# A selective-scan block with du*B made by TensorE and most of the weighing by C on GpSimd

## The chip, the cores and the metric

One core of a Trainium2 chip runs the kernel. The time is the device time of the whole program in microseconds; the profile is of one execution on the same core. The engines are TensorE (PE, its weight loads PEld), VectorE (DVE), ScalarE (ACT), GpSimd (POOL) and SyncE (SP), which issues the DMAs.

## The reference

For 4 sequences of 256 steps: a selective state-space layer (256 channels, 16 states each) that is gated by the normalised x and added to x, and then a feed-forward layer with ternary weights and 8-bit activations. The layer that the change is about, with `hidden` the context (128 numbers a step) and z the layer-normalised x:

```python
x = einsum('ed,bld->bel', in_proj_w, hidden)
u = silu(conv4(x) + conv_b)                        # depthwise, 4 taps
x_dbl = einsum('ke,bel->bkl', x_proj_w, u)         # 8 of dt, 16 of B, 16 of C
delta = softplus(dt_proj_w @ dt_lo + dt_proj_b)
dA = exp(d_t[..., None] * A)
state = state * dA + (d_t * u_t)[..., None] * B_t[:, None, :]     # for each t
y_t = einsum('ben,bn->be', state, C_t)
y = (y + D * u) * silu(z)
```

The output is x1 + ffn(layernorm(x1)), with x1 = x + y. All of the scan is in f32.

## The kernel before

The sequences are done in two groups (g) of two (b), so that a row of W = 512 numbers is two sequences of 256 steps. The 256 channels are two halves (eh) of 128 partitions. For each group there are 16 states times 2 halves, UNITS = 32 scan units, and so 64 in all; unit i has state i // 2 and half i % 2.

A unit passes four engines. **ACT** makes the decay exp(delta * A) in one of three PSUM banks (`decays`, L653; its first column in each sequence is zero, so that one scan instruction does both sequences). **POOL** makes the drive du * B for both halves of a state in one instruction of 1024 columns (`scan_drive`, L491), where B's row was spread over the partitions by a DMA from DRAM (`b_wide`). **DVE** runs the scan (`scan`, L898), an instruction of 512 columns. The state is then weighed by C's row: for 22 of the 32 states DVE does it (`weigh`, L908, 512 columns, against `cwide`, a PSUM bank that **PE** fills from three bf16 parts of C, `spread_c`, L1177), and for the ten states of POOL_C GpSimd does it (`weigh`, L501, 1024 columns, C's row by DMA). PE adds the weighed states to `ysum`, two PSUM banks with the time steps on the partitions, by four f32 transposes of 128 columns for each unit (`add_to_y`, L1156). At the end of a group DVE multiplies `ysum` by silu(z) and x is added (`gate_and_add`).

Softplus goes by proj on PE, ACT's abs, exp, relu and ln (`softplus_parts`), and four DVE or POOL operations (`deltas`, `softplus`, `deltas_rest`). DVE splits C in three parts (`split_c`). While the units of both groups run, the engines also do the conv and projections of group 1, the ternary weights (ACT rounds, PE turns, ACT copies, DVE clips: `weight_rows`, `clip_weights`) and the feed-forward layer of group 0, at unit numbers that are written out in the lists ahead of the program (PE_ROWS, PE_GATE, DVE_VAL and so on). After the last scan come the gate of group 1, its feed-forward layer, and what is left of group 0's. Each engine runs its instructions in the order of the program; work waits by semaphores, and a bank of PSUM is filled again when its read is counted (`work_tile`, `wait_read`).

## Time and profile before

| | |
|---|---|
| time, median of 3 runs | 228.26 us (226.56 to 228.98) |
| span of the profiled execution | 224.8 us |
| busy, share of the span | PE 67%, DVE 83%, POOL 61%, ACT 58% |
| mean granted clock of TensorE | 0.803 |
| first and last scan start | 26.9 us and 184.4 us |

The busy time of an engine is the time in which one of its instructions ran. A duration of PE holds its latency, so the pace of PE is read from the starts of consecutive groups. The granted clock 0.5 is 1.2 GHz and 1.0 is 2.4 GHz. An f32 matmul that isn't a transpose stands as two instructions in the trace. Idle time counts only on the engine that sets the end.

### The profile page before, as it was taken

How to read it: one execution, taken by the hardware profiler on the slowest of the kernel's cores; microseconds unless marked ns; L12 is line 12 of the kernel's file. 1: busy time of each engine (PE TensorE's matmuls, PEld its weight loads, DVE VectorE, ACT ScalarE, POOL GpSimd, SP SyncE). 2: the span in 40 equal slices, each digit the busy share in tenths (PEclk: the TensorE clock that was granted, in tenths of full speed). 3: DMA queues.
4: the chain of work that ended last, by engine and by line, in shares of the span. 5: the costliest groups of instructions: out<-in, count | busy, mean ns of one | idle time of the engine just before them, and what ended most of it. 6: DMA issues, size and time to landing. Idle time of an engine off the chain costs nothing.

```text
span 224.8 us, 2405 instructions
## 1 busy us (share of the span) xinstructions
PE 150.9 (67%) x706; PEld 92.9 (41%) x706; DVE 186.5 (83%) x284; ACT 129.3 (58%) x197; POOL 136.8 (61%) x132
## 2 busy tenths in 40 slices
PE   6983088643979197059630777926986667899983
PEld 5531054232636186048620533504435265334552
DVE  3789999998089999999999968797869998838661
ACT  2578675336585996076341758736498015376772
POOL 5036499778900999896685999999139202691000
PEclk9995559978585769758785596985589969999999
DMA  4894943261400223004003304314000000000002
GB/s 107 231 343 123 339 146 112 87 189 42 140 13 0 75 66 92 4 0 141 0 0 98 135 3 136 73 71 140 23 1 3 23 0 0 0 28 0 23 23 70
DMA packets 12689, 17.44 MB, mean 78 GB/s; under 512 B 3468, under 2 KB 9012, under 8 KB 12678
## 3 DMA queue, kind: packets, MB, share of 16 engines
q1 hardware_dynamic: 12678, 17.30, 24.5%
q8 instruction: 5, 0.08, 0.2%
q14 instruction: 6, 0.05, 0.1%
HBM read 16.11 MB, written 1.19 MB: 77 GB/s over the span
## 4 chain that ended last, share of the span: by engine, by line
DVE 19%; PE 16%; ACT 9%; issue 6%; POOL 5%; DVEq 0%; POOLq 0%; ACTq 0%
DVE wstate L908 3%; PE work L1242 2%; DVE state L898 2%; PE work L1282 2%; DVE gam L981 2%; DVE xhat L825 2%; PE decay L1067 2%; ACT decay L653 2%; DVE pool_state L898 2%; DVE wstage L976 2%; POOL drive L491 2%; ACT gT L722 2%; ACT wstage L703 1%; PE decay L1242 1%; PE work L1249 1%
## 5 line engine op out<-in xcount | busy, mean ns | idle before, releaser
L491 POOL TENSOR_TENSOR drive<-du,b_wide 128x1024 f32<-128x1024 f32 x31 | 74.2, 2407 | 2.9 <-DVE state L898 1.8
L653 ACT ACTIVATE decay<-delta,aneg 128x510 f32<-128x510 f32 x64 | 42.9, 684 | 45.9 <-DVE state L898 23.3
L898 DVE TENSOR_TENSOR_SCAN state<-decay,drive 128x512 f32<-128x512 f32 x44 | 52.4, 1208 | 0.9 <-issue 0.9
L1156 PE MATMUL ysum<-ident,wstate 128*128 128x128 f32 x176 | 32.9, 332 | 10.6 <-DVE wstate L908 10.6
L908 DVE TENSOR_TENSOR wstate<-state,cwide 128x512 f32<-128x512 f32 x44 | 29.1, 663 | 12.2 <-issue 11.8
L1156 PEld LDWEIGHTS ysum<-ident,wstate 128*128 128x128 f32 x176 | 26.1, 172 | 18.8 <-DVE wstate L908 13.8
L501 POOL TENSOR_TENSOR pool_wstate<-pool_state,c_wide 128x1024 f32<-128x1024 f32 x10 | 23.7, 2367 | 11.4 <-PE ysum L1156 8.6
L898 DVE TENSOR_TENSOR_SCAN pool_state<-decay,drive 128x512 f32<-128x512 f32 x20 | 24.3, 1214 | 0.2 <-ACT decay L653 0.2
L1067 PE MATMUL work<-ident,wstage 128*128 128x128 f32 x80 | 14.2, 331 | 11.4 <-ACT ternary L677 7.7
L1177 PE MATMUL cwide<-cparts,sel 128*128 128x512 bf16 x22 | 10.6, 483 | 15.4 <-DVE wstate L908 14.2
L1067 PEld LDWEIGHTS work<-ident,wstage 128*128 128x128 f32 x80 | 11.8, 174 | 12.7 <-ACT ternary L677 8.1
L1242 PE MATMUL work<-ternary,qT 128*128 128x512 bf16 x46 | 16.3, 445 | 1.1 <-DVE wstage L976 0.8
L1156 PE MATMUL ysum<-ident,pool_wstate 128*128 128x128 f32 x80 | 13.3, 322 | 1.6 <-POOL pool_wstate L501 1.6
L716 ACT ACTIVATE wstage<-wstage,gam 128x512 f32<-128x512 f32 x16 | 10.6, 716 | 6.0 <-DVE gam L984 6.0
L509 POOL TENSOR_TENSOR xhat<-xhat,x_in 128x1024 f32<-128x1024 f32 (+1 forms) x2 | 3.6, 1814 | 16.0 <-DVE xhat L926 12.5
L1156 PEld LDWEIGHTS ysum<-ident,pool_wstate 128*128 128x128 f32 x80 | 11.9, 171 | 2.7 <-POOL pool_wstate L501 1.9
L976 DVE SCALAR_TENSOR_TENSOR wstage<-work,gam,wstage 128x512 f32<-128x512 f32 x12 | 8.7, 744 | 4.8 <-ACT wstage L703 3.4
L1067 PE MATMUL work<-ident,xhat 128*128 128x128 f32 x24 | 6.2, 420 | 9.6 <-ACT xhat L689 5.9
L1177 PEld LDWEIGHTS cwide<-cparts,sel 128*128 128x128 bf16 x22 | 2.5, 112 | 20.4 <-DVE wstate L908 17.6
L1156 PE MATMUL ysum<-ident,skip 128*128 128x128 f32 x16 | 3.0, 352 | 10.7 <-issue 8.7
L981 DVE TENSOR_REDUCE gam<-wstage 128x1 f32<-128x1024 f32 x8 | 9.8, 1220 | 0.3
L1249 PE MATMUL work<-bias_rows,acol 9*128 9x512 bf16 x23 | 9.8, 432 | 0.0
(180 smaller groups left out, 298.7 us busy)
## 6 DMA issues: line engine op xcount, KB each, us to landing
b_wide<-bc_rows SPq DMA_DIRECT2D x16, 512.0 KB, 4.5
c_wide<-bc_rows SPq DMA_DIRECT2D x10, 256.0 KB, 3.5
x_in<-in_x SPq DMA_DIRECT2D x2, 512.0 KB, 4.9
wstage<-in_L_ffn_gate_w SPq DMA_DIRECT2D x1, 1024.0 KB, 7.8
wstage<-in_L_ffn_val_w SPq DMA_DIRECT2D x1, 1024.0 KB, 10.3
wstage<-in_L_ffn_out_w SPq DMA_DIRECT2D x1, 1024.0 KB, 9.0
ctx_in<-in_ctx SPq DMA_DIRECT2D x2, 256.0 KB, 4.4
out<-wtap SPq DMA_DIRECT2D x4, 128.0 KB, 1.7
```

Source lines behind the costliest of these rows:

```text
L491: nc.gpsimd.tensor_tensor(drive[:, m % NDR], du[:, m // NS], rows.unsqueeze(1).to_broadcast([P, EH, W]), ALU.mult).then_inc(s_drive, 1)
L501: nc.gpsimd.tensor_tensor(pool_wstate[:], pool_state[:, k % NPS], c_wide[:, k % 2].unsqueeze(1).to_broadcast([P, EH, W]), ALU.mult).then_i ...
L653: nc.scalar.activation(v[:, :, 1:L], d[:, :, 1:L], ACT.Exp, scale=aneg[:, eh, n:n + 1]).then_inc(s_decay, 1)
L898: nc.vector.tensor_tensor_scan(dst, decay[i % ND][:], drive[:, i // EH % NDR, i % EH], 0.0, ALU.mult, ALU.add).then_inc(s_scan, 1)
L908: nc.vector.tensor_tensor(wstate[:, rank(i) % NWS], state[:, rank(i) % NST], cwide[:], ALU.mult).then_inc(s_wst, 1)
L976: release(nc.vector.scalar_tensor_tensor(v, bank[:], gam[:, 3, t:t + 1], v, ALU.mult, ALU.mult), name)
L981: link(nc.vector.tensor_reduce(gam[:, 5, t:t + 1], gv[:, t], axis=AX.X, op=ALU.max, apply_absolute_value=True))
L1067: return nc.tensor.matmul(dst, lhsT=src, rhs=ident[0:src.shape[0], 0:src.shape[0]], start=True, stop=True, is_transpose=True, **flags)
L1156: last = nc.tensor.matmul(ysum[:, k, eh * P:(eh + 1) * P], lhsT=src[:, k * P:(k + 1) * P], rhs=ident[:], start=start and k % LB == 0, stop ...
L1177: nc.tensor.matmul(cwide[:], lhsT=sel[:, m % NS], rhs=cparts[:, m // NS], start=True, stop=True).then_inc(s_cwide, 1)
L1242: nc.tensor.matmul(bank[:], lhsT=qT[:, d, t * P:(t + 1) * P], rhs=wT[:, d, cols], start=d == 0, stop=False)
L1249: fill(nc.tensor.matmul(banks[TILE[name][0]], lhsT=acol[rows, t * P:(t + 1) * P], rhs=bias_rows[rows, cols], start=False, stop=True), name)
```

## The change

The scan units are cut otherwise. A slot is a pair of states for one half of the channels (32 slots), and a unit is one sequence of a slot: one scan instruction of 512 columns runs two states of 256 steps. There are 64 units as before.

- The drive is made by PE, in four PSUM banks: du is turned (`turn_du`, duT has time on the partitions), and multiplied with a diagonal matrix of B (`drives`: for each unit two f32 matmuls, one per block of 128 steps, of 256 columns). The diagonals are made by POOL, by one select of 1024 columns for each pair of states (`diagonals`, 16 in all). Decays go to SBUF.
- The weighing is on POOL (`weigh`, 1024 columns for a slot, 28 of the 32 slots), C's rows by DMA (16 of 512 KB); slots 7, 15, 23 and 31 are weighed by DVE, 1024 columns each. `spread_c` and `split_c` are gone.
- The sum is no transpose any more: `ysum` has channels on the partitions, and PE adds a slot by two f32 matmuls of 512 columns with the identity (`sums`). The D * u term is a matmul with a diagonal of D (`skips`). The gated y is turned at a group's end (`turn_y`).
- Softplus: dt's two projections are folded in one matrix (`wd`), `pre_delta` is two f32 matmuls of 512 columns over 128 rows where it was one over 8 rows, and the four terms of delta are added by PE with four f32 matmuls (`add_delta`); DVE keeps relu, one rounding and du.
- silu(z) is made by ACT straight from x (8 instructions `silu_x`), with no turned z; the normalising of x on DVE (8) and the turning on PE (16) are gone. The clips of the weights are gone (ACT uses Sign). `scales` is two small DVE instructions where it was three.
- The lists of positions are new; the group loads of x and the load of val_w stand later in SP's order.

The core of the diff:

```diff
-POOL_C = (2, 5, 8, 13, 17, 19, 21, 24, 26, 28)
-POOL_WAIT, SUM_WAIT = 3, 6
...
+NP = NS // 2
+SLOTS = NP * EH
+UNITS = SLOTS * BG
+ORDER = [(0, 0), (1, 0), (0, 1), (1, 1)] + [(p, eh) for p in range(2, NP) for eh in range(EH)]
+NSLOT = G * SLOTS
+NUNIT = G * UNITS
+ND = 4
+NDRV = 4
+NST = 3
+NPW = 2
+NDG = 3
+NCW = 3
+DVE_SLOTS = tuple(range(7, NSLOT, 8))
+DRIVE_LEAD = 3
+SUM_LAG = 5
...
+        decay = sb("decay", [P, ND, BG, 2, L])
...
+        drive = [pb(f"drive{i}", [P, BANK]) for i in range(NDRV)]
+        banks = [work[0][:], work[1][:], ysum[:, 0], ysum[:, 1], *(d[:] for d in drive)]
...
+            def load_c(k):
+                if k >= NCW:
+                    for eh in range(EH):
+                        wait_weighed(sp, slot_of((k - NCW) // NP, (k - NCW) % NP, eh))
+                rows = c_rows[k].rearrange("b n l -> (b n l)").rearrange("(a w) -> a w", a=1).to_broadcast([P, BG * 2 * L])
+                sp.dma_start(c_wide[:, k % NCW].rearrange("p b n l -> p (b n l)"), rows).then_inc(s_cload[k % NCW], 16)
...
+            def diagonals(k):
+                g, p = divmod(k, NP)
+                if p == 0:
+                    wait_read(pool, f"bt{g}")
+                if k >= NDG:
+                    pool.wait_ge(s_drive, BG * last_slot(k - NDG) + BG)
+                values = bt[:, g, p].rearrange("p t n -> p (t n)")
+                nc.gpsimd.affine_select(out=bdiag[:, k % NDG].rearrange("p t n l -> p (t n) l"),
+                                        in_=values.unsqueeze(2).to_broadcast([P, GT * 2, P]),
+                                        compare_op=ALU.is_equal, fill=0.0, base=0, pattern=[[0, GT * 2], [-1, P]],
+                                        channel_multiplier=1).then_inc(s_diag, 1)
...
+            def weigh(s):
+                g, p, _ = slot_parts(s)
+                k = g * NP + p
+                r = pool_rank(s)
+                pool.wait_ge(s_scan, BG * s + BG)
+                pool.wait_ge(s_cload[k % NCW], 16 * (k // NCW + 1))
+                if r >= NPW:
+                    pool.wait_ge(s_ysum, s - NPW + 1)
+                nc.gpsimd.tensor_tensor(flat(pool_wstate[:, r % NPW]), flat(state[:, s % NST]), flat(c_wide[:, k % NCW]),
                                         ALU.mult).then_inc(s_poolw, 1)
...
+            diagonals(0)
+            diagonals(1)
+            split_biases()
+            for s in range(NSLOT):
+                if s % EH == 0 and s // EH + 2 < G * NP:
+                    diagonals(s // EH + 2)
+                if s not in DVE_SLOTS:
+                    weigh(s)
...
+            t = wait_full(act, "wd")
+            release(nc.scalar.activation(wdT[:].rearrange("p h e -> p (h e)"), t[:], ACT.Copy), "wd")
             act.wait_ge(s_small, 16 * 4)
...
+                if i == 3:
+                    copy_delta(0, 1)
+                    turned_du(0, 1)
+                    taps(1)
...
+                nc.scalar.activation(decay[:, s % ND, :, n, 1:L], d[:, :, 1:L], ACT.Exp,
+                                     scale=aneg[:, eh, 2 * p + n:2 * p + n + 1]).then_inc(s_decay, 1)
...
+            def make_du(g, eh):
+                t = wait_full(dve, f"dl{g}{eh}")
+                wait_u(dve, g, eh)
+                if g:
+                    wait_full(dve, f"dut0{eh}")
+                nc.vector.tensor_tensor(du[:, eh], t[:], u[:, eh], ALU.mult).then_inc(s_du, 1)
...
+                nc.vector.tensor_tensor_scan(state[:, s % NST, b].rearrange("p n l -> p (n l)"),
+                                             decay[:, s % ND, b].rearrange("p n l -> p (n l)"), drive[i % NDRV][:], 0.0,
                                              ALU.mult, ALU.add).then_inc(s_scan, 1)
...
+            def weigh(s):
+                g, p, _ = slot_parts(s)
+                k = g * NP + p
+                dve.wait_ge(s_scan, BG * s + BG)
+                dve.wait_ge(s_cload[k % NCW], 16 * (k // NCW + 1))
+                if dve_rank(s):
+                    dve.wait_ge(s_ysum, DVE_SLOTS[dve_rank(s) - 1] + 1)
+                flat = lambda v: v.rearrange("p b n l -> p (b n l)")
+                nc.vector.tensor_tensor(flat(wstate[:]), flat(state[:, s % NST]), flat(c_wide[:, k % NCW]),
                                         ALU.mult).then_inc(s_wst, 1)
...
+            def gate(g, b):
+                if b == 0:
+                    dve.wait_ge(s_ysum, SLOTS * (g + 1))
+                    dve.wait_ge(s_xs, GT * (g + 1))
+                z = xs[:, g * GT + b * LB:g * GT + (b + 1) * LB]
+                nc.vector.tensor_tensor(yg[:, :, b], ysum[:, :, b * L:(b + 1) * L], z, ALU.mult).then_inc(s_gated, 1)
...
+            def scales(row, src, t0, t1, done):
+                link(nc.vector.tensor_scalar(gam[:, src, t0:t1], gam[:, src, t0:t1], FLOOR, 1.0 / QMAX, ALU.max, ALU.mult))
+                nc.vector.reciprocal(gam[:, row, t0:t1], gam[:, src, t0:t1]).then_inc(done, 1)
...
+            positive(0, 0)
+            positive(0, 1)
+            t = wait_full(dve, "bc0")
+            release(nc.vector.tensor_copy(proj[:], t[0:2 * NS, :]), "bc0")
+            rounded(0, 0)
+            make_du(0, 0)
+            release(nc.vector.tensor_copy(delta[:, 0, 0], wait_full(dve, "dl00")[:]), "dl00")
+            rounded(0, 1)
+            t = wait_full(dve, "dut00")
+            release(nc.vector.tensor_copy(duT[:, 0, :, 0], t[:].rearrange("p (t e) -> p t e", t=GT)), "dut00")
+            make_du(0, 1)
...
-            def add_to_y(src, g, eh, start):
-                for k in range(GT):
-                    last = nc.tensor.matmul(ysum[:, k, eh * P:(eh + 1) * P], lhsT=src[:, k * P:(k + 1) * P],
-                                            rhs=ident[:], start=start and k % LB == 0, stop=True,
-                                            is_transpose=True, skip_group_check=True)
-                return last
...
+            def add_delta(g, eh):
+                name = f"dl{g}{eh}"
+                t = work_tile(name)
+                pe.wait_ge(s_relu, EH * g + eh + 1)
+                nc.tensor.matmul(t[:], lhsT=ident[:], rhs=relu[:, eh], start=True, stop=False)
+                pe.wait_ge(s_expln, 2 * (EH * g + eh) + 1)
+                nc.tensor.matmul(t[:], lhsT=ident[:], rhs=mag[:, eh], start=False, stop=False)
+                pe.wait_ge(s_back, EH * g + eh + 1)
+                nc.tensor.matmul(t[:], lhsT=nident[:], rhs=back[:, eh], start=False, stop=False)
+                pe.wait_ge(s_expln, 2 * (EH * g + eh) + 2)
+                fill(nc.tensor.matmul(t[:], lhsT=ident[:], rhs=lnw[:, eh], start=False, stop=True), name)
...
+            def skips(g):
+                if g:
+                    pe.wait_ge(s_gated, BG * g)
+                else:
+                    pe.wait_ge(s_ddiag, 1)
+                for eh in range(EH):
+                    wait_u(pe, g, eh)
+                    last = nc.tensor.matmul(ysum[:, eh], lhsT=ddiag[:, eh], rhs=u[:, eh], start=True, stop=True,
+                                            skip_group_check=True)
+                last.then_inc(s_skips, 1)
...
+            def drives(i):
+                s, b = divmod(i, BG)
+                g, p, eh = slot_parts(s)
+                k = g * NP + p
+                if i >= NDRV:
+                    pe.wait_ge(s_scan, i - NDRV + 1)
+                if p == 0 and b == 0:
+                    wait_read(pe, f"dut{g}{eh}")
+                pe.wait_ge(s_diag, k + 1)
+                bank = drive[i % NDRV][:].rearrange("p (n l) -> p n l", n=2)
+                for c in range(LB):
+                    t = b * LB + c
+                    last = nc.tensor.matmul(bank[:, :, c * P:(c + 1) * P], lhsT=duT[:, g, t, eh], rhs=bdiag[:, k % NDG, t],
+                                            start=True, stop=True)
+                last.then_inc(s_drive, 1)
...
+            def sums(s):
+                _, _, eh = slot_parts(s)
+                wait_weighed(pe, s)
+                src = wstate[:] if s in DVE_SLOTS else pool_wstate[:, pool_rank(s) % NPW]
+                for n in range(2):
+                    last = nc.tensor.matmul(ysum[:, eh], lhsT=ident[:], rhs=src[:, :, n], start=False, stop=True,
+                                            skip_group_check=True)
+                last.then_inc(s_ysum, 1)
...
-            project(0)
+            t = work_tile("wd")
+            wait_read(pe, "dtw")
+            for k in range(EH):
+                last = nc.tensor.matmul(t[:, k * DI:(k + 1) * DI], lhsT=xproj[0:DR, k * P:(k + 1) * P],
+                                        rhs=dtwT[:].rearrange("p h e -> p (h e)"), start=True, stop=True)
+            fill(last, "wd")
             pre_delta(0, 0)
             pre_delta(0, 1)
+            project(0)
+            taps(1)
+            add_delta(0, 0)
+            turn_b(0)
+            turn_du(0, 0)
+            add_delta(0, 1)
+            turn_du(0, 1)
             context(1)
-            spread_c(0)
-            for name in ("pre01", "ctx1"):
+            for name in ("bt0", "wd", "xc00", "conv1"):
+                wait_read(pe, name)
+            for i in range(DRIVE_LEAD):
+                drives(i)
+            for name in ("dut01", "ctx1"):
                 wait_read(pe, name)
             skips(0)
             for i in range(PE_OUT[-1] + 1):
-                scan_step(i)
+                if i + DRIVE_LEAD < NUNIT:
+                    drives(i + DRIVE_LEAD)
+                if i >= SUM_LAG and (i - SUM_LAG) % BG == 0:
+                    s = (i - SUM_LAG) // BG
+                    if s < NSLOT - 1:
+                        if s == SLOTS:
+                            skips(1)
+                        sums(s)
                 if i < EH * TAPS:
...
+            for s in range((PE_OUT[-1] - SUM_LAG) // BG + 1, NSLOT):
+                sums(s)
+            for b in range(BG):
+                turn_y(1, b)
```

## Rows read from the trace of the kernel before

**Rows 1.** Windows: busy us of each engine, granted clock (PEclk), DMA; scans, tail, three PE stretches.

```profile
core 0: us, PE busy (x) PEld busy (x) DVE busy (x) ACT busy (x) POOL busy (x), PEclk, DMA share, GB/s
27.00:186.00 159.00, 102.30 (x467) 66.97 (x467) 140.96 (x178) 90.49 (x131) 115.80 (x69) 0.75 0.21 67
186.00:224.80 38.80, 32.52 (x187) 17.18 (x187) 24.85 (x59) 22.61 (x39) 11.07 (x37) 1.00 0.06 21
8.60:12.00 3.40, 3.40 (x11) 1.42 (x10) 3.29 (x7) 3.06 (x7) 0.00 (x0) 1.00 0.87 250
30.60:34.00 3.40, 3.40 (x6) 1.15 (x6) 3.40 (x5) 1.56 (x3) 3.40 (x3) 0.50 0.01 0
57.00:71.00 14.00, 12.54 (x38) 7.60 (x38) 8.20 (x15) 8.43 (x13) 4.68 (x4) 0.62 0.19 60
```

**Rows 2.** The page, part 5: costliest groups (busy, mean ns, idle before them).

```profile
L491 POOL TENSOR_TENSOR drive<-du,b_wide 128x1024 f32<-128x1024 f32 x31 | 74.2, 2407 | 2.9 <-DVE state L898 1.8
...
L898 DVE TENSOR_TENSOR_SCAN state<-decay,drive 128x512 f32<-128x512 f32 x44 | 52.4, 1208 | 0.9 <-issue 0.9
L1156 PE MATMUL ysum<-ident,wstate 128*128 128x128 f32 x176 | 32.9, 332 | 10.6 <-DVE wstate L908 10.6
L908 DVE TENSOR_TENSOR wstate<-state,cwide 128x512 f32<-128x512 f32 x44 | 29.1, 663 | 12.2 <-issue 11.8
...
L501 POOL TENSOR_TENSOR pool_wstate<-pool_state,c_wide 128x1024 f32<-128x1024 f32 x10 | 23.7, 2367 | 11.4 <-PE ysum L1156 8.6
L898 DVE TENSOR_TENSOR_SCAN pool_state<-decay,drive 128x512 f32<-128x512 f32 x20 | 24.3, 1214 | 0.2 <-ACT decay L653 0.2
```

**Rows 3.** Timeline, start-up: start us, us, instruction.

```profile
8.56 3.60 PE L1119 MATMUL ysum<-ctxT,wtapT 128*128 128x512 f32 x8
...
12.20 0.69 ACT L729 ACTIVATE u<-ysum,convb 128x512 f32<-128x512 f32 x1
...
12.90 1.28 ACT L730 ACT_TABLE_LOAD   x1
...
26.94 1.22 DVE L898 TENSOR_TENSOR_SCAN state<-decay,drive 128x512 f32<-128x512 f32 x1
```

**Rows 4.** Timeline of PE, 30.5 to 35 us: two taps, four instructions.

```profile
30.57 3.62 PE L1119 MATMUL work<-ctxT,wtapT 128*128 128x512 f32 x4
33.99 0.63 PE L1177 MATMUL cwide<-cparts,sel 128*128 128x512 bf16 x1
```

**Rows 5.** Timeline of PE, 104 to 107 us: 128-column transposes.

```profile
104.54 1.04 PE L1156 MATMUL ysum<-ident,pool_wstate 128*128 128x128 f32 x8
105.42 1.04 PE L1156 MATMUL ysum<-ident,wstate 128*128 128x128 f32 x8
```

**Rows 6.** Timeline of PE, 198 to 212 us: one bank of the feed-forward layer.

```profile
201.49 0.60 PE L1242 MATMUL cwide<-ternary,qT 128*128 128x512 bf16 x2
202.03 0.39 PE L1249 MATMUL cwide<-bias_rows,acol 9*128 9x512 bf16 x1
202.35 0.61 PE L1242 MATMUL work<-ternary,qT 128*128 128x512 bf16 x2
```

**Rows 7.** Instruction groups kept apart by shape: selects on POOL.

```profile
L424 POOL TENSOR_SCALAR_AFFINE_SELECT pick<-pick 128x16 bf16<-128x16 bf16 x3 | 0.6, 198 | 0.4
...
L418 POOL TENSOR_SCALAR_AFFINE_SELECT ident<-ident 128x128 f32<-128x128 f32 x1 | 0.3, 292 | 0.2 <-POOL ident L417 0.2
```

**Rows 8.** Timeline of DVE, 19 to 40 us: an operation, freely and held up.

```profile
30.36 0.48 DVE L825 TENSOR_SCALAR xhat<-x_in,mv,nv 128x256 f32<-128x256 f32 x1
...
35.33 2.56 DVE L825 TENSOR_SCALAR xhat<-x_in,mv,nv 128x256 f32<-128x256 f32 x1
```

**Rows 9.** Chain of work that ended last, 186 to 190 us: start us, us, what.

```profile
186.29 1.27 PE ysum L1156 x8
...
187.58 1.30 DVE xhat L926 x2
...
188.91 1.26 DVE xhat L930
```

More of the change, by code:

```diff
@@ L133, in work_tiles, with place @@
     tiles, used = {}, [0] * 8
-    for names, banks in ((first, (0, 1, 2, 3)), (scans, (0, 1)), (last, (4, 5, 6, 7, 0, 1))):
+    def place(name, bank):
+        tiles[name] = (bank, used[bank])
+        used[bank] += 1
+    for name, bank in first.items():
+        place(name, bank)
+    for names, banks in ((scans, (0, 1)), (last, (4, 5, 6, 7, 0, 1))):
         for i, name in enumerate(names):
-            bank = banks[i % len(banks)]
-            tiles[name] = (bank, used[bank])
-            used[bank] += 1
+            place(name, banks[i % len(banks)])
     return tiles
@@ L1001, in _ @@
+            make_du(0, 0)
[4 more added lines that the diff above has]
+            make_du(0, 1)
+            for i in range(NUNIT):
                 scan(i)
-                if i and not on_pool(i - 1):
-                    weigh(i - 1)
+                if i % BG == BG - 1 and i // BG in DVE_SLOTS:
+                    weigh(i // BG)
@@ L1122, in convolve_tap, with pre_delta @@
                     fill(last, name)
+            def pre_delta(g, eh):
+                name = f"pre{g}{eh}"
+                t = work_tile(name)
+                if g == 0:
+                    wait_read(pe, "wd")
+                for k in (1, 0):
+                    wait_u(pe, g, k)
+                    last = nc.tensor.matmul(t[:], lhsT=wdT[:, k, eh * P:(eh + 1) * P], rhs=u[:, k], start=k == 1,
+                                            stop=k == 0)
+                fill(last, name)
             def project(g):
-                name = f"proj{g}"
+                name = f"bc{g}"
                 t = work_tile(name)
```

801 lines of the change are left out of this document (333 added, 468 removed).

## The prediction

> **What bounds the kernel now.** I read the windows first. In the 159 us of the scans VectorE is busy for 141 us, GpSimd for 116, TensorE for 102 and ScalarE for 90; TensorE has a mean granted clock of 0.75 there [rows 1]. So VectorE sets the pace, and TensorE has 57 us without work, and much of its work at the low clock. The costliest groups say what VectorE does: 64 scans of 1.21 us (52.4 + 24.3 = 77 us) and 44 weighings (29.1 us); GpSimd's large items are 31 drives of 2.41 us and 10 weighings of 2.37 us [rows 2]. The scans begin at 26.9 us [rows 3]. The last sums on TensorE end at 187.6 us and the gate of group 1 begins [rows 9]; 37.2 us of feed-forward work follow, with the clock at 1.00.
>
> **TensorE's part of the change, the term that decides.** The price of an f32 matmul that is no transpose comes from the conv taps. Each tap, a matmul of 512 columns, stands as two instructions. At the low clock (0.50 from 30.6 to 34 us [rows 1]) the four instructions of two taps start at 30.57 us and the next work starts at 33.99 [rows 4]: 3.42 us, 1.71 us a tap. At the full clock (1.00 from 8.6 to 12 us [rows 1]) the eight instructions of four taps take 3.60 us, the latency of the last included [rows 3]; half of 1.71 gives 4 x 0.855 = 3.42 us and leaves 0.18 for it. So a matmul of 512 columns costs 0.86 us at the full clock, weight loads included, and by columns one of 256 costs 0.43 us.
>
> The part that is in the loop for each of the 64 units:
> - drives, two of 256 columns: 64 x 2 x 0.43 = 55.0 us;
> - sums, two of 512 for each of 32 slots: 32 x 2 x 0.86 = 55.0 us.
>
> What they replace: 256 transposes of 128 columns, 0.11 us each at the full clock (104.54 to 105.42 us is eight [rows 5]), 28 us, and 22 spreads of C.
>
> The Trainium skill (TensorE: Matmul & The Clock Gate, Terms) puts transpose mode at 4 times the f32 speed, which speaks against this change, since it gives up the transposes. Here 128 columns cost 0.11 us with it and 0.214 us without, twice, not four times; by the rule, with the transposes' row as its base, the sums would be 32 x 2 x 1.76 = 113 us and the whole 58 us longer. The rows for the very instruction decide, so I use 0.86.
>
> The rest that TensorE does between the first drive and the last sum, at full clock:
> - 0.86 us each: 8 taps of group 1, 4 for `skips`, 4 in `pre_delta(1)`, 2 for `project(1)`, 8 in `add_delta(1)`: 26 x 0.86 = 22.4 us;
> - 0.11 us each: 48 transposes of weights, 24 of the hidden rows, 28 for B, du, y, the quantised rows and scales: 100 x 0.11 = 11.0 us;
> - 16 banks of gate and val for group 0: 201.49 to 202.35 is one, 0.86 us [rows 6]: 13.8 us;
> - 24 bf16 matmuls of 256 columns for three output tiles, half of 0.29: 3.4 us.
>
> The sum is 110 + 22.4 + 11.0 + 13.8 + 3.4 = 160.6 us. This is work on one engine in order, and there is no slack in it: it is as long as the whole scan stage of before (159 us), even at clock 1.00 and without one stall. **TensorE becomes the bound.**
>
> **The other engines lie below it.** VectorE: of its 141 busy us [rows 1] the 44 weighings of 29 us go [rows 2], which leaves 112; four of 1024 columns come, 2 x 0.66 = 1.3 us each if free and up to 3.4 us when GpSimd is in the way (below), so 117 to 126 us. Of its other edits those that go (clips, C's parts, the normalising of x, most of softplus) outweigh those that come, so this is an upper bound. GpSimd: 28 weighings of 2.37 us = 66 us; the selects: 16 columns took 0.198 and 128 took 0.292 us [rows 7], which by the slope (0.84 ns a column) is 1.05 us for 1024, and in proportion to 128 columns 2.3 us, so 16 are 17 to 37 us. I take 1.1, the slope being between two rows of the same operation. The 116 us of before less its drives (74) and weighings (24) leave 18 us of other work, so GpSimd has 101 to 121 us. ScalarE's 90 us change by a few copies of 0.7 us that come and go. GpSimd's work for a pair of states, 1.75 x 2.37 + 1.1 = 5.3 us (6.4 with the dear select), is under TensorE's 4 x 1.72 = 6.9 us for it, and a sum is issued five units after its scan, some 8 us, against 2.4 us for the weighing. So these are covered; without the cover GpSimd would set the pace with 121 us at most, still below 160. C's rows are 16 loads; nothing on SP stands ahead of them but `vw`, `ow` and the bias spread, as before.
>
> On the four weighings on VectorE: one operation took 0.48 us freely and 2.56 us when GpSimd held the port [rows 8]. The Trainium skill (GPSIMD Engine Reference, Specifications) names two SBUF inputs as such a case. That is up to 4 x 2.1 = 8 us of VectorE, and it lies under TensorE's 160; TensorE is covered by the three units of drives made ahead (5 us), so only the weighing at the very end is on the path, +0.7 us.
>
> **The start.** Before, u is ready at 12.9 us and the first scan starts at 26.94 [rows 3]. Now: TensorE makes `wd` after the taps (12.0 to 12.9), and ScalarE copies it ahead of both silus, each of the three 0.7 us by the silu's row, so u is ready at 15.0. Then `pre_delta(0,0)` 0.86 behind the last u, `pre_delta(0,1)` 1.7, `project(0)` 1.7, four turns 0.5: 19.9 us. `add_delta(0,0)` 4 x 0.86 ends at 23.4; du on VectorE, four turns on TensorE 24.8; `add_delta(0,1)` 3.4 ends at 28.2; du 0.7, turns 0.6; on ScalarE the copy of du 0.6 and then `taps(1)` 0.6, on which the drives wait: first drive at 30.9, first scan at 31.8 us, 4.9 us later than before. If this stretch falls to the low clock in half of its f32 work (12 us), it is 6 us more. Above all VectorE's long work there is gone, but it doesn't help: the chain goes through TensorE's twelve f32 matmuls.
>
> **The end.** Gate, one set of turns and add are 0.65 + 0.5 + 0.7 for the first half where it was 1.30 + 1.26 [rows 9] for both; one small operation less in `scales` (0.17 us) two or three times on the chain. The four-unit lead means that the last sums follow the last scans with a 1.3 us weighing and 1.7 us of sums where it was 0.67 + 1.27; these sums are in the 160.6. Together -0.5 us against 37.2.
>
> **The sum.** First drive at 31, plus 160.6 with 4.5% for handoffs at which TensorE waits (two work banks only; ScalarE's read between): 168 us, ends at 199. Before it was 187.6. So +11.4 - 0.5 = +11 us: a span of 236 us against 224.8. The median of the runs is 3.5 us over the span, so the time is 239 us.
>
> **The rivals.**
> 1. Same bound, but at a poor clock. TensorE at 90% busy in 57 to 71 us had a clock of 0.62 [rows 1]. If a tenth to a quarter of the 160 us runs at the low clock, it is 16 to 40 us more: 252 to 276. Against it: a fed TensorE is at 1.00 in the tail and at 8.6 us. Chance 0.16.
> 2. Faster, by VectorE's relief: the f32 columns on TensorE overlap more than the taps show, or the drives cost less than by columns. VectorE then sets the pace at some 120 us of work plus 10% waits = 132; from 31 the sums end at 163: 24.6 us off, -0.5, that is a time of 203 us. It decides from the point where TensorE's stage falls under 188.1 - 31 = 157 us with its waits, 150 without: of the 132.4 us that go at 0.86, ten must go, so from 0.79 us per 512 columns on there is a gain, and from 0.73 one of 10 us. Only the taps' price at two clocks speaks against it, but that is firm. Chance 0.11.
> 3. GpSimd binds: a weighing at 2.4 us plus a select of over 2.8 us, or held up by VectorE. 28 x 2.4 + 16 x 4 + 18 = 149 us is still below; it must combine with its in-order waits (a select waits for drives three pairs back, and sums wait for the weighing). Price: 10 us over the forecast, 249. Chance 0.08.
> 4. No change: fewer stalls (1%) and a first scan at 29 us: 29 + 162 = 191, +3.4 - 0.5 = +3, a time of 231, at the edge of 1%. Chance 0.07.
>
> The forecast itself, 233 to 250, has 0.58. A measurement can't tell less than about 1% from nothing. Slower by over 1%: 0.58 + 0.16 + 0.08 + part of rival 4 = 0.84; same 0.05; faster 0.11. The range leaves out the faster case and the worst of the clock: 230 to 258 us.
>
> **What would show it.** In the new profile TensorE should be busy over 90% of the scan stage at a clock of 0.95 to 1.00, with 0.86 us a unit for drives and as much for sums; VectorE's scans should wait for TensorE's drives, some 0.5 us each; its share falls under 70%. The first scan at 31 to 34 us, the last at 193 to 200. GpSimd's select near 1.1 us. The prediction is wrong if drive matmuls start less than 0.4 us apart at the full clock, if VectorE still has no idle time, or if the clock stays near 0.75.

## The result, and the profile after

| | before | after |
|---|---|---|
| time, median of 4 runs beside each other | 227.79 us (226.56 to 228.98) | 244.28 us (243.43 to 245.79) |
| span of the profiled execution | 224.8 us | 243.3 us |
| first drive on TensorE, first scan | first scan 26.9 us | 31.95 us, 33.19 us |
| end of the last sums on TensorE | 187.6 us | 204.9 us |

The ratio of after to before is 1.078, with an interval of 1.070 to 1.086: the change makes the kernel 7.8% slower. The forecast was 239 us, and 230 to 258. Some executions, of before above all, fell in a slower state with a lower clock: the medians of this table hold them, the ratios and all times further down leave them out.

The page of the kernel after: busy time by engine, and two rows of its 40 slices (tenths).

```profile
span 243.3 us, 2683 instructions
...
PE 222.3 (91%) x868; PEld 127.7 (52%) x868; DVE 147.1 (60%) x212; ACT 130.3 (54%) x200; POOL 106.8 (44%) x124
...
PE   7979779999999999999997569999999998699984
...
PEclk9999999999999999999999979999999999979999
```

TensorE is busy almost without a break, at a mean clock of 0.99; in before it was at 67% of the span, and at a clock of 0.75 in the scans [rows 1]. VectorE fell from 83% to 60%.

Windows of after (columns as in [rows 1]); the second to sixth cover the scans, the last is the tail.

```profile
core 0: us, PE busy (x) PEld busy (x) DVE busy (x) ACT busy (x) POOL busy (x), PEclk, DMA share, GB/s
32.00:60.00 28.00, 27.69 (x96) 17.88 (x97) 19.47 (x32) 21.26 (x31) 15.96 (x11) 1.00 0.22 78
60.00:100.00 40.00, 40.00 (x137) 23.14 (x136) 24.92 (x23) 24.41 (x35) 19.35 (x11) 1.00 0.12 45
100.00:140.00 40.00, 36.00 (x153) 24.35 (x151) 26.58 (x31) 16.41 (x26) 24.32 (x14) 1.00 0.19 61
140.00:180.00 40.00, 37.33 (x138) 20.79 (x139) 27.88 (x34) 23.09 (x36) 21.30 (x26) 0.96 0.13 44
180.00:205.00 25.00, 24.39 (x96) 12.46 (x94) 13.85 (x21) 11.54 (x16) 9.43 (x4) 1.00 0.02 6
205.00:243.00 38.00, 30.92 (x167) 15.81 (x167) 23.10 (x52) 18.85 (x34) 9.98 (x36) 0.96 0.06 21
```

From 32 to 205 us TensorE is busy for 165.4 of 173 us. VectorE has 112.7 us there where it had 140.96, GpSimd 90.4 where it had 115.8 [rows 1].

The page of after, part 5 (as [rows 2]).

```profile
L473 POOL TENSOR_TENSOR pool_wstate<-state,c_wide 128x1024 f32<-128x1024 f32 x28 | 66.6, 2380 | 73.6 <-PE ysum L1159 64.4
L865 DVE TENSOR_TENSOR_SCAN state<-decay,drive 128x512 f32<-128x512 f32 x64 | 75.2, 1206 | 21.7 <-PE drive L1149 21.1
L1149 PE MATMUL drive<-bdiag,duT 128*128 128x256 f32 x256 | 65.8, 388 | 7.1 <-DVE state L865 6.0
...
L1159 PE MATMUL ysum<-pool_wstate,ident 128*128 128x512 f32 x112 | 53.8, 603 | 0.0
...
L458 POOL TENSOR_SCALAR_AFFINE_SELECT bdiag<-bt 128x1024 f32<-128x1024 f32 x16 | 18.9, 1182 | 17.3 <-ACT bt L590 17.3
```

The scans are as long as they were, 1.21 us. GpSimd's 41 operations of 2.4 us [rows 2] have become 28, and 16 selects of 1.18 us. For 64 us GpSimd waits for a sum, that is, for a buffer to come free.

The chain of work that ended last, in after, while the first units run: start us, us, what.

```profile
38.77 0.86 PE drive L1149 x4
39.64 0.86 PE work L1065 x2
...
45.66 0.86 PE drive L1149 x4
46.52 1.72 PE ysum L1159 x4
```

The chain here is TensorE's own order and nothing else. Four instructions of a unit's drive take 0.86 us, and the four of a slot's sums 1.72 us.

### The profile page after: what moved, and what is told of

Same layout as the page of the kernel before. It is cut to its first block, busy times and chain, and to the rows that moved or that the text cites. A ratio compares the mean times of both kernels' runs of the same rounds, so it can differ in the third digit from the quotient of the medians.

```text
span 243.3 us, 2683 instructions
## 1 busy us (share of the span) xinstructions
PE 222.3 (91%) x868; PEld 127.7 (52%) x868; DVE 147.1 (60%) x212; ACT 130.3 (54%) x200; POOL 106.8 (44%) x124
## 4 chain that ended last, share of the span: by engine, by line
PE 79%; DVE 12%; ACT 4%; issue 3%; DMA 1%; ACTq 0%; SPq 0%; DVEq 0%
PE ysum L1159 20%; PE drive L1149 20%; PE work L1035 5%; PE work L1222 3%; PE drive L1035 3%; DVE state L865 3%; PE work L1078 3%; PE work L1065 3%; PE drive L1222 2%; DVE mag L802 2%; PE work L1229 2%; PE work L1265 2%; PE ysum L1132 2%; PE drive L1065 1%; PE work L1113 1%
## 5 line engine op out<-in xcount | busy, mean ns | idle before, releaser
L473 POOL TENSOR_TENSOR pool_wstate<-state,c_wide 128x1024 f32<-128x1024 f32 x28 | 66.6, 2380 | 73.6 <-PE ysum L1159 64.4
L865 DVE TENSOR_TENSOR_SCAN state<-decay,drive 128x512 f32<-128x512 f32 x64 | 75.2, 1206 | 21.7 <-PE drive L1149 21.1
L1149 PE MATMUL drive<-bdiag,duT 128*128 128x256 f32 x256 | 65.8, 388 | 7.1 <-DVE state L865 6.0
L1149 PEld LDWEIGHTS drive<-bdiag,duT 128*128 128x128 f32 x256 | 46.7, 191 | 27.0 <-issue 14.8
L1159 PE MATMUL ysum<-pool_wstate,ident 128*128 128x512 f32 x112 | 53.8, 603 | 0.0
L1159 PEld LDWEIGHTS ysum<-pool_wstate,ident 128*128 128x128 f32 x112 | 21.6, 195 | 16.0 <-issue 14.7
L458 POOL TENSOR_SCALAR_AFFINE_SELECT bdiag<-bt 128x1024 f32<-128x1024 f32 x16 | 18.9, 1182 | 17.3 <-ACT bt L590 17.3
L641 ACT ACTIVATE ternary<-work,negmagic 128x512 bf16<-128x512 f32 x12 | 7.6, 685 | 8.9 <-PE work L1035 8.9
L667 ACT ACTIVATE wstage<-work,gam 128x512 f32<-128x512 f32 x12 | 8.0, 680 | 1.2 <-PE work L1229 0.8
L1078 PE MATMUL work<-u,wdT 128*128 128x512 f32 x16 | 7.3, 597 | 1.4 <-ACT u L699 1.4
```

The lines of the kernel that those rows point to most:

```text
L458: nc.gpsimd.affine_select(out=bdiag[:, k % NDG].rearrange("p t n l -> p (t n) l"), in_=values.unsqueeze(2).to_broadcast([P, GT * 2, P]), c ...
L473: nc.gpsimd.tensor_tensor(flat(pool_wstate[:, r % NPW]), flat(state[:, s % NST]), flat(c_wide[:, k % NCW]), ALU.mult).then_inc(s_poolw, 1)
L865: nc.vector.tensor_tensor_scan(state[:, s % NST, b].rearrange("p n l -> p (n l)"), decay[:, s % ND, b].rearrange("p n l -> p (n l)"), driv ...
L1078: last = nc.tensor.matmul(t[:], lhsT=wdT[:, k, eh * P:(eh + 1) * P], rhs=u[:, k], start=k == 1, stop=k == 0)
L1149: last = nc.tensor.matmul(bank[:, :, c * P:(c + 1) * P], lhsT=duT[:, g, t, eh], rhs=bdiag[:, k % NDG, t], start=True, stop=True)
L1159: last = nc.tensor.matmul(ysum[:, eh], lhsT=ident[:], rhs=src[:, :, n], start=False, stop=True, skip_group_check=True)
```

## The experiments

Times are medians. The kernel before took 225.3 to 227.0 us beside each group of them, and after was not run again beside them, so a difference of 1 us from after means little. "Stage" is the time from the first drive on TensorE to the end of the last sums, as the start of the gate shows it; for after it is 31.95 to 204.90, 172.9 us.

### Is it TensorE, and how much of its work comes back as time?

**e1_half_sums** makes one of the two sum matmuls of each slot.

```diff
-                for n in range(2):
+                for n in range(1):
                     last = nc.tensor.matmul(ysum[:, eh], lhsT=ident[:], rhs=src[:, :, n], start=False, stop=True,
```

> Left out: the second state of each pair isn't added to y (one f32 matmul of 512 columns per slot instead of two), so 32 of TensorE's matmuls at 0.86 us = 27.5 us are gone; everything else runs as in the changed kernel. Theory (TensorE is the bound of the scan stage): the time falls by 21 to 28 us, to 216 to 223 us, the loss against 27.5 being places where TensorE waited already. Rival (VectorE's holds or the order of the waits set the pace, and TensorE's busy time only fills it): less than 8 us. Rival (GpSimd's weighing is the pace): no change.

It took 224.95 us, 19 less than after, where 21 to 28 were expected. Taking 27.5 us of matmuls from TensorE, with no change to any other engine's work, gives 19 us: TensorE's own work is the bound, but 8 us don't come back.

**e4_transposed_sums** has the arithmetic of after, in f32, with the sum made as before: time on the partitions and eight transposes of 128 columns for a slot. z is turned instead of y. VectorE's block at the change of groups also stands two units earlier than in after; e11, below, puts it back.

```diff
-                    last = nc.tensor.matmul(ysum[:, eh], lhsT=ident[:], rhs=src[:, :, n], start=False, stop=True,
-                                            skip_group_check=True)
+                    for t in range(GT):
+                        b, c = divmod(t, LB)
+                        last = nc.tensor.matmul(ysum[:, t, eh * P:(eh + 1) * P], lhsT=src[:, b, n, c * P:(c + 1) * P],
+                                                rhs=ident[:], start=False, stop=True, is_transpose=True,
+                                                skip_group_check=True)
```

> The changed kernel with the sums as before: ysum has time on the partitions and each slot is added by eight f32 transposes of 128 columns (8 x 0.11 = 0.88 us) instead of two f32 matmuls of 512 (1.72 us); z is turned (16 transposes, four copies on ScalarE) instead of y. TensorE has 32 x 0.84 = 27 us less. Theory (TensorE binds, f32 matmuls that are no transposes are the cost): 20 to 27 us faster than the changed kernel, 217 to 224 us, so faster than the kernel before. Rival (the transposes cost as much, their weight loads being on the path): within 4 us of 244. Rival (after TensorE's relief VectorE's holds bind at once): 232 to 238 us.

229.54 us, 15 less than after, between the 20 to 27 of the theory and the 6 to 12 of the second rival, and 1.018 of before (1.007 to 1.028). The sums of one slot in e4's chain of work:

```profile
71.33 0.87 PE ysum L1178 x8
```

A slot's sums take 0.87 us where after needs 1.72: some 27 us of work are gone. 12 of them don't come back as time. The windows of e4, from 60 us on, show where a part of them went:

```profile
60.00:110.00 50.00, 49.34 (x283) 38.88 (x282) 36.77 (x32) 37.61 (x57) 28.32 (x16) 1.00 0.19 64
110.00:122.00 12.00, 8.79 (x49) 7.66 (x49) 9.66 (x15) 2.23 (x4) 7.99 (x6) 0.86 0.00 0
122.00:150.00 28.00, 22.40 (x119) 16.28 (x118) 19.39 (x20) 16.31 (x25) 18.09 (x23) 0.94 0.21 75
```

To 110 us TensorE still has no gap. From 110 to 150 us it stands idle for 8.8 of 40 us, and its clock is down. After is idle for 6.0 us in the same window, at a clock of 0.96, so this is only a part of the 12. Behind 150 us TensorE waits for 4.4 us more, for steps of the feed-forward layer (3.5 us) and for the last weighing on VectorE (0.9 us); in after the waits of this kind are 1.1 us. The window from 110 us on is the change of groups, and VectorE's timeline says what it did there:

```profile
111.33 1.29 DVE L904 TENSOR_TENSOR lnw<-ysum,xs 128x512 f32<-128x512 f32 x2 [1.94 <-PE ysum L1178]
112.54 3.33 DVE L911 TENSOR_TENSOR lnw<-lnw,x_in 128x512 f32<-128x512 f32 x2
```

The two additions of x, with both inputs in SBUF, took 3.33 us. After does the same additions from a PSUM bank, 128.19 us and 1.29 for both (below). The scan after them starts at 117.66 us, 6.3 us after the gate began.

**e5_bf16_drives** rounds du and B to bf16 for the drives alone, so its output is less exact.

```diff
-        bdiag = sb("bdiag", [P, NDG, GT, 2, P])
+        bdiag = sb("bdiag", [P, NDG, GT, 2, P], BF16)
...
-        duT = sb("duT", [P, G, GT, EH, P])
+        duT = sb("duT", [P, G, GT, EH, P], BF16)
```

> The turned du and the diagonals of B are bf16 tiles (so du and B are rounded to bf16; nothing is left out), the drives' matmuls are one bf16 instruction of 256 columns where they were two of f32. By columns and the f32 pace (0.43 us for 256) against 0.11 to 0.14 us, TensorE has 128 x 0.30 = 38 us less. The first test took away 27.5 us and gave 19 us, so theory (TensorE's f32 passes are the cost, but its relief is used up at the group change, where VectorE holds): 22 to 30 us faster, 214 to 222 us. Rival (two thirds of TensorE's relief always come through, no other limit): 218 and no new waits on VectorE. Rival (the drives' matmuls are hidden behind the sums): under 5 us.

219.76 us, 24.5 less than after, and 0.974 of before (0.967 to 0.981). The window of e5 at the change of groups:

```profile
110.00:122.00 12.00, 3.40 (x13) 1.23 (x12) 11.83 (x19) 3.96 (x8) 8.21 (x11) 0.85 0.23 87
```

VectorE is busy for all 12 us of it and TensorE for 3.4: the bound has changed hands in this place.

**e9_both** has the edits of e4 and e5 together.

> Sums by transposes and drives from bf16 operands together (du and B rounded to bf16, nothing left out). TensorE has 27 + 38 = 65 us less than in the changed kernel. Alone they gave 15 and 24.5 us. Theory (once TensorE is relieved the scans go at VectorE's pace, with its blocks at the group change and the feed-forward chain of group 0 as limits): the second relief is worth only 5 to 12 us more than the larger alone, 208 to 215 us. Rival (the gains add up, TensorE still being the bound): 203 to 206 us. Rival (something else binds already): 217 to 220 us.

216.7 us (215.3 and 218.1, two runs only), 3 below e5, and between the 208 to 215 of the theory and the 217 to 220 of the last rival. With 15 and 24.5 us for each edit alone and 27.6 for both, the second relief of some 27 us brings 3: over most of the stage TensorE is not the bound any more after the first. What sets the rest isn't shown by a trace.

### Do VectorE or GpSimd bind?

**e2_dve_every_fourth** gives VectorE eight weighings in place of four.

```diff
-DVE_SLOTS = tuple(range(7, NSLOT, 8))
+DVE_SLOTS = tuple(range(3, NSLOT, 4))
```

> Slots 3, 7, 11 ... (8 of 32) are weighed by VectorE instead of 4: GpSimd has 4 x 2.38 = 9.5 us less, VectorE 4 x 1.43 = 5.7 us more. Theory (TensorE binds): within 1.5 us of the changed kernel, 243 to 246 us. Rival (GpSimd's pace matters): 4 to 9 us faster. Rival (VectorE's pace matters): 3 to 6 us slower.

243.21 us, 1.1 below after, a difference that these few runs hardly tell from none. Four weighings of 2.38 us moved, and the stage took 172.65 us where after's took 172.95. The whole span of its profiled execution is 1.9 us shorter, and 1.65 of that is in the tail, which the edit doesn't touch (see "The end" below). Its group of weighings:

```profile
L473 POOL TENSOR_TENSOR pool_wstate<-state,c_wide 128x1024 f32<-128x1024 f32 x24 | 57.2, 2383 | 81.5 <-PE ysum L1159 71.3 <-DVE state L865 10.3
```

GpSimd waits longer (71.3 us for sums, where after has 64.4): it was given less, and had to wait for TensorE all the same.

**e3_second_select** issues every select twice, the first into a spare buffer.

```diff
+                nc.gpsimd.affine_select(out=spare[:].rearrange("p t n l -> p (t n) l"),
+                                        in_=values.unsqueeze(2).to_broadcast([P, GT * 2, P]),
...
```

> Each of the 16 selects of 1024 columns on GpSimd is issued twice, the first into a spare tile: 16 x 1.18 = 18.9 us more on GpSimd. Theory (TensorE binds, GpSimd idle for 70 us in waits for sums): 0 to 2 us slower; the first two selects stand beside work of the start. Rival (GpSimd's work is on the path): 10 to 19 us slower.

247.22 us, 3 over after: more than the 0 to 2 of the theory, and far from the 10 to 19 of the rival. The waits for sums, in after and then in e3:

```profile
POOL pool_wstate L473 <- PE ysum L1159: 64.4, 23, 8.1
...
DVE state L865 <- PE drive L1149: 21.1, 12, 3.5
```

```profile
POOL pool_wstate L480 <- PE ysum L1166: 51.1, 18, 6.0
```

GpSimd's busy time rose from 106.8 to 124.4 us, and 13 of these 18 went into time in which GpSimd waited anyway. The stage is 174.0 us, 1.1 over after's, and the whole span of the profiled execution, 244.9 us, is 1.6 over. Where the rest of the 3 us comes from stays open.

### Can the waits at the change of groups be taken away?

**e7_spread_after** spreads the additions of x, the statistics and the normalising of group 0 over units 38 to 44, where they were in two blocks.

```diff
-DVE_GATED, PE_YT, DVE_X1, DVE_INPUT = 36, 38, 38, 41
-ACT_RND, PE_COLS, ACT_COLS = 42, 45, 46
+DVE_GATED, PE_YT, DVE_INPUT = 36, 38, 44
+DVE_ADD, DVE_STATS, DVE_NORM = (38, 39), (39, 40), (41, 42, 43, 44)
+ACT_RND, PE_COLS, ACT_COLS = 45, 46, 46
```

> The changed kernel with VectorE's work at the group change (two additions of x, statistics, four normalisings) spread over units 38 to 44 where it was at 38 and 41 in two blocks; the rounding and turning behind it moved to unit 45 and 46. Theory (TensorE stalls some 8 us at 131 to 142 us because VectorE's blocks of 3 and 6 us are longer than the lead of three drives): 4 to 8 us faster, 237 to 240 us. Rival (the scans only catch up later, TensorE's idle time there is refilled elsewhere): within 1.5 us of 244.

250.85 us, 6.6 over after; I had expected 4 to 8 less. In the trace the stage is 3.9 us longer. The waits of TensorE's drives for scans did shrink, from 6.0 to 3.5 us. Timeline of TensorE in e7, a little later:

```profile
154.29 0.81 PE L1041 MATMUL work<-ident,apart 128*41 128x128 f32 x4 [3.40 <-POOL apart L498]
156.31 0.63 PE L1228 MATMUL work<-ternary,qT 128*128 128x512 bf16 x1 [1.21 <-ACT acol L660]
```

The chain of the feed-forward layer (normalise, maximum, scales, columns) now ends later, TensorE comes to its columns at their fixed place in its order, and waits there with the drives queued behind: 4.6 us where after has none. From 150 to 170 us TensorE is busy for 15.2 of 20 us. (2 of the 5.6 us of longer span are at the start: the first drive was at 33.92 us in this execution. From 14.95 to 20.15 us the eight instructions of `pre_delta` ran at a mean clock of 0.70; they took 5.20 us where after's took 3.67 at 1.00.)

**e8_spread_transposed** does the same to e4.

> The version with sums by transposes (229.5 us) with the same spreading, over units 36 to 44. It was 15 us faster than the changed kernel, not 27, and TensorE stood idle some 12 us at 111 to 129 us, when VectorE held. Theory: 6 to 12 us faster than without, 218 to 223 us, below the kernel before. Rival (the wait there is the chain of gate, sums and weighing at the group's end and not VectorE's blocks): 227 to 231 us.

232.15 us, 2.6 over e4, just over the rival's 227 to 231. It is wrong in the same way: in its trace TensorE waits 2.88 us for the scales ahead of the columns and 1.21 for the columns, where e4 waits 0.52 for the first and not for the second. And there was less to win than the expectation says: e4's two waits for scans at this place are 3.21 and 4.87 us, 8.1 and not 12.

**e11_transposed_late** leaves e4's blocks whole, and sets them two units later, as in after (the edit is against e4).

```diff
-DVE_GATED, DVE_X1, DVE_INPUT = 36, 36, 39
+DVE_GATED, DVE_X1, DVE_INPUT = 36, 38, 41
```

> The version with sums by transposes, with VectorE's additions of x at unit 38 and the normalising at 41, where the changed kernel has them, in place of 36 and 39. Spreading that block with a later end made it slower, since the feed-forward chain began later. Theory (the chain's begin counts most): 1 to 4 us slower than 229.5. Rival (the block at 36, of gate, additions and statistics in one, is the hold that costs): 2 to 5 us faster.

226.59 us, 2.9 below e4 and equal to before (0.999, 0.992 to 1.005): the rival was right, not the theory. So some 3 of the 12 us that e4 didn't get back were of the place of this one block. With the block where after has it, the transposes alone are worth 17.7 of their 27 us. In f32 that is as far as the redesign came: no gain over the kernel before.

### What are the edits worth that don't touch TensorE?

**e6_before_sign** is the kernel before, in which ScalarE rounds and clips the ternary weights in one step by Sign, and VectorE's clips are gone.

```diff
-                release(nc.scalar.activation(dst, t[:], ACT.Copy, bias=-MAGIC), name)
+                release(nc.scalar.activation(dst, t[:], ACT.Sign, bias=negmagic[:]), name)
...
-                if i in DVE_CLIP:
-                    clip_weights(DVE_CLIP.index(i))
```

> The kernel before with one part of the change alone: the ternary weights are clipped by ScalarE's Sign as they leave PSUM, and VectorE's three clips of 2048 columns (4.1 us) are gone. Theory (before, VectorE was the bound of the scans): 2 to 4 us faster than before. Rival (these clips stood in VectorE's waits or Sign costs a table load each time): within 1 us or slower.

222.90 us, 0.988 of before (0.981 to 0.995), some 3 us less.

**e10_before_sign_silu** adds that ScalarE makes silu of the normalised x straight from x; VectorE's eight normalisings are gone.

```diff
+                    for t in range(B * LB):
+                        nc.scalar.activation(xhat[:, t], x_in[:, t], ACT.Silu, bias=nv[:, 2, t:t + 1],
+                                             scale=nv[:, 1, t:t + 1]).then_inc(s_xhat, 1)
...
-                if 1 <= i <= B * LB:
-                    normalise(xhat, x_in, i - 1, i, s_xhat)
```

> The kernel before with two parts of the change: the clips by Sign (measured alone: 4 us faster than before), and silu(z) made by ScalarE from x before it is turned, so VectorE's eight normalisings of x (7.6 us) are gone. Theory (VectorE bound before): 3 to 6 us faster than with Sign alone, 217 to 220 us. Rival (ScalarE's block of ten instructions at unit 14 delays decays as much): 222 to 226 us.

217.4 us, 5.5 less than e6. Its window, to be read against the first of [rows 1]:

```profile
27.00:186.00 159.00, 104.75 (x505) 67.69 (x514) 138.90 (x187) 98.01 (x145) 118.08 (x78) 0.80 0.19 65
```

The scans of e10 end earlier, so this window holds 8 us of its tail. From its first scan to the end of its last sums (26.34 to 177.97 us, 151.6 us) VectorE is busy for 132.1 us, and in before for 141.9 of 160.6: it stays the bound, and of 9.8 us taken from it 9.0 come back as time.

**e12_before_three_parts** adds the shorter `scales`.

```diff
-                link(nc.vector.tensor_scalar(gam[:, src, t0:t1], gam[:, src, t0:t1], FLOOR, None, ALU.max))
-                link(nc.vector.reciprocal(gam[:, row, t0:t1], gam[:, src, t0:t1]))
-                last = nc.vector.tensor_scalar(gam[:, row, t0:t1], gam[:, row, t0:t1], QMAX, None, ALU.mult)
+                link(nc.vector.tensor_scalar(gam[:, src, t0:t1], gam[:, src, t0:t1], FLOOR, 1.0 / QMAX, ALU.max, ALU.mult))
+                nc.vector.reciprocal(gam[:, row, t0:t1], gam[:, src, t0:t1]).then_inc(done, 1)
```

> The kernel with the two parts (Sign, silu of x by ScalarE; 217.6 us) and a third of the change: the scale of a token is one VectorE operation shorter, and in the feed-forward layer it is given out ahead of the dequantising factor (two operations of 0.16 and 0.21 us off the chain of each tile). Theory (in the tail each tile's maximum, scale and rounding are a chain that the end hangs on for some of the tiles): 1 to 2.5 us faster, 215 to 216.6 us. Rival (TensorE is busy in the tail, and the chain is covered): within 0.5 us of 217.6.

216.12 us (214.94 to 217.01), 0.955 of before (0.949 to 0.962). It is the fastest version here that keeps all of before's f32, some 10 us under before and 28 under after. So the change holds two things: small edits that take work from VectorE and are worth some 10 us on the old kernel, and the rest, the new cut of the scan with the softplus on TensorE, which costs more than they bring. The two halves of this rest were not measured apart.

## Why the prediction was right

**The bound.** It named TensorE, and e1, e11 and e5 show it: less of TensorE's work alone makes the kernel 18 to 24.5 us faster, while e2 and e3 move GpSimd's load both ways for 1 to 3 us. The signs asked for are there: 96% busy in the stage (165.4 of 173), a clock of 0.96 to 1.00, and the first and last scans at 33.2 and 199.7 us. The scans' waits for drives are 21.1 us, a third of a microsecond for each of the 64, but they stand in 12 waits of up to 3.5 us and not before every scan; the text said some 0.5 each. VectorE and GpSimd had less work in the stage than the text gave them (112.7 us against 117 to 126, 90.4 against 101 to 121), so both lay further below TensorE.

**The price.** 0.86 us for an f32 matmul of 512 columns, and 0.43 for 256, came from two taps at the low clock and four at the full one [rows 3, 4]. The chain of after has just that. The Trainium skill (TensorE: Matmul & The Clock Gate, Terms) makes transpose mode 4 times as fast for FP32. e4 doesn't agree: its transposes take 0.87 us for what took 1.72, twice. The select took 1.18 us where 1.1 was said.

**The start.** 31.8 us was said for the first scan, and it was 33.19. Timeline of after:

```profile
24.04 0.69 DVE L854 TENSOR_TENSOR du<-work,u 128x512 f32<-128x512 f32 x1 [3.01 <-PE work L1113]
...
28.97 0.69 DVE L854 TENSOR_TENSOR du<-work,u 128x512 f32<-128x512 f32 x1 [2.32 <-PE work L1113]
...
30.97 0.59 ACT L551 ACTIVATE wtapT<-drive 128x512 f32<-128x512 f32 x1
...
31.95 2.40 PE L1149 MATMUL drive<-bdiag,duT 128*128 128x256 f32 x10 [1.08 <-ACT wtapT L551]
33.19 1.22 DVE L865 TENSOR_TENSOR_SCAN state<-decay,drive 128x512 f32<-128x512 f32 x1 [3.53 <-PE drive L1149]
```

The order is that of the prediction, step by step. The first du starts at 24.04 us where 23.4 was said, and the second at 28.97 where 28.2 was, so most of the delay is there before the sums of delta are done for the first half. The first drive is at 31.95 where the text had 31, and the scan follows 1.24 us later where 0.9 was said. It is the smallest of the misses.

**The handoffs, the step that was sized too low.** The 160.6 us of work were to take 168 with 4.5% of waits; the stage took 172.9, so the allowance is 7.7%, 12.3 us. TensorE's records show 7.6 us idle in it, and 6.0 of these are two waits for scans at the change of groups. The low clock behind the second adds 1.8 us (below); some 3 us are left, and where they lie stays open. VectorE there, and then TensorE: start us, us, instruction [idle before <- releaser].

```profile
128.19 1.29 DVE L896 TENSOR_TENSOR lnw<-work,x_in 128x512 f32<-128x512 f32 x2 [2.93 <-PE work L1035]
...
131.26 3.41 DVE L865 TENSOR_TENSOR_SCAN state<-decay,drive 128x512 f32<-128x512 f32 x3
134.59 4.54 DVE L802 TENSOR_SCALAR mag<-lnw,mv,nv 128x256 f32<-128x256 f32 x4
139.17 1.22 DVE L923 TENSOR_REDUCE gam<-mag 128x4 f32<-128x1024 f32 x1
...
140.73 5.67 DVE L865 TENSOR_TENSOR_SCAN state<-decay,drive 128x512 f32<-128x512 f32 x5
```

```profile
132.50 2.24 PE L1149 MATMUL drive<-bdiag,duT 128*128 128x256 f32 x8 [1.33 <-DVE state L865]
134.58 1.88 PE L1159 MATMUL ysum<-pool_wstate,ident 128*128 128x512 f32 x4
136.30 1.03 PE L1149 MATMUL drive<-bdiag,duT 128*128 128x256 f32 x4
142.01 1.81 PE L1149 MATMUL drive<-bdiag,duT 128*128 128x256 f32 x4 [4.68 <-DVE state L865]
143.61 2.94 PE L1159 MATMUL ysum<-pool_wstate,ident 128*128 128x512 f32 x4
146.38 1.89 PE L1149 MATMUL drive<-bdiag,duT 128*128 128x256 f32 x8
```

The four normalisings took 4.54 us, 1.1 each, where one is free at 0.48 [rows 8]; GpSimd was busy beside them. With the maximum behind them no scan began from 134.6 to 140.7 us. I had counted on three units of drives made ahead, 5 us on TensorE, and held this against the four weighings, where it was enough. The two blocks on group 0's x1 were not in the text at all, neither the additions with their statistics (3.1 us, 128.19 to 131.26) nor the normalising with the maximum (6.1 us). The second is longer than the lead, and the lead was no longer whole: only three scans stand between the blocks, and when the second began TensorE had one slot's sums and one unit's drives left to do, 2.6 us. The normalising was in the kernel before too, and nearly as slow (VectorE's timeline of before):

```profile
116.97 4.15 DVE L825 TENSOR_SCALAR xhat<-xhat,mv,nv 128x256 f32<-128x256 f32 x4
```

But VectorE was then the bound, and the time stood in its own sum. Under the new bound it is a wait of TensorE. That the waits would go if the blocks did is argued from these rows; e7, which spread them, only moved the wait.

What came behind the wait is seen in four windows of after:

```profile
132.00:137.00 5.00, 4.50 (x16) 2.87 (x16) 5.00 (x7) 2.66 (x4) 4.54 (x4) 1.00 0.21 56
137.50:142.00 4.50, 0.00 (x0) 0.00 (x0) 4.40 (x6) 1.16 (x3) 2.51 (x6) 1.00 0.09 30
142.00:146.30 4.30, 4.29 (x8) 2.51 (x9) 4.30 (x4) 2.85 (x6) 1.66 (x10) 0.60 0.01 4
146.30:150.00 3.70, 3.70 (x15) 2.40 (x14) 2.55 (x3) 0.36 (x1) 3.28 (x2) 1.00 0.00 0
```

For 4.5 us TensorE had nothing, and then it ran at a mean clock of 0.60. Four drive instructions took 1.60 us (142.01 to 143.61) and four of sums 2.77 (to 146.38), where they take 0.86 and 1.72: 1.8 us more. So the one wait cost some 6.5 us, more than the whole stage's miss against the forecast. The table carries the same sum for the others (stage as defined above, work as summed in the prediction less what the edit takes away):

| kernel | stage | work of TensorE | difference |
|---|---|---|---|
| after | 172.9 | 160.6 | 12.3 |
| e1 | 150.5 | 133.1 | 17.4 |
| e4 | 156.3 | 133.4 | 22.9 |
| e11 | 153.9 | 133.4 | 20.5 |
| e5 | 148.8 | 119.5 | 29.3 |

e5's 128 matmuls for drives are taken at a price from TensorE's timeline in e4, where eight bf16 matmuls of 256 columns go before the next work in 0.87 us; so 13.9 us stand for 55.0:

```profile
184.33 1.03 PE L1286 MATMUL work<-ternary,gT 128*128 128x256 bf16 x8
185.20 1.04 PE L1178 MATMUL ysum<-ident,pool_wstate 128*128 128x128 f32 x8
```

The difference holds idle time and low clock alike; of idle time alone TensorE has 7.5 us in after's stage, 14.5 in e4's and 21.8 in e5's. The less TensorE has to do, the more of it turns into waits for the others. Relief of the bound was worth 0.55 to 0.7 of its size (15 of 27 us in e4, 18 in e11, 19 of 27.5 in e1), not all of it.

**The end.** 36.7 us was said, and it took 38.4. Windows of after's tail:

```profile
205.00:215.00 10.00, 7.00 (x34) 3.48 (x35) 8.17 (x23) 1.50 (x3) 4.87 (x20) 0.95 0.04 13
215.00:225.00 10.00, 9.97 (x48) 4.28 (x46) 5.76 (x9) 6.19 (x13) 5.11 (x18) 0.88 0.00 0
225.00:235.00 10.00, 10.00 (x56) 4.94 (x56) 6.08 (x15) 7.72 (x14) 0.00 (x0) 1.00 0.09 29
```

Before had a clock of 1.00 here [rows 1]. A mean of 0.88 and 0.95 over 10 us each means 2.4 and 1.0 us at half the clock, and so 1.7 us of work lost: as much as the miss. Two other runs bear it out: e2 and e5 have the same tail, at a clock of 1.00 in their traces, and it took 36.75 and 36.77 us, the 36.7 of the forecast. Rival 1 (a poor clock) came true in this small way only. Its price is also too low by 3 us: the 16 to 40 us were added to the span of 236 and not to the time of 239.

**The sum.** Start +1.0, stage +4.9, tail +1.7 make 243.3 from the 235.7 us that the steps gave (rounded to 236). The time is 1.0 us over this span and not 3.5, which gives back 2.5: 244.3 against 239. That last term was luck. The 3.5 set the median of before against the span of a quick execution (an execution of 226.88 us had a span of 224.9, 2.0 less), so it held some 1.5 us of spread between runs. The other misses are all of one sign, and the main term, 160.6 us of work on one engine, held.

## What to carry to other kernels

Before work moves to an engine that looks idle, price it at that engine's full clock and add up all that the engine then does in order: here 160.6 us stood against a stage of 159. An engine that becomes the bound inherits every block that the others did unseen; a lead made ahead must be longer than the longest block (6.1 us here, against 5), and blocks that stand close together draw on the same lead (three scans between them here). And a redesign should be taken apart: three small edits of this one, on the old kernel, gave 4.5%, while the whole made it 7.8% slower.

## What was not expected of the hardware

After 4.5 us without work TensorE's next 4.3 us ran at a mean clock of 0.60, so that the gap cost more than its length; in the window with the 1.33 us gap ahead of 132.5 it was 1.00. VectorE's f32 operations from SBUF were slow where GpSimd worked beside them: four normalisings took 4.54 us in after, where one took 0.48 [rows 8], and two additions with both inputs in SBUF 3.33 us in e4, where the same two with one input in PSUM took 1.29 us in after, with GpSimd busy as well. That GpSimd is the cause is read from its being busy at the time; no run took its work away. GpSimd's own instruction, 2.38 us, was hardly longer than before's 2.37 [rows 2].
